# Attention output of an adaLN block: PV product in four column groups of 256 queries, normalised after a trip through DRAM

## The reference

```python
h = _layernorm(x) * (1 + ca) + sa
q, k, v = projections of h with bias, 16 heads of 16 features, q scaled by 0.25
scores = einsum('bihd,bjhd->bhij', q, k) + slopes * -|i - j|
probs = softmax(scores)                      # over the 1024 keys
out = einsum('bhij,bjhd->bihd', probs, v)    # the PV product
x = x + ga * (out @ Wo.T + bo)
h = _layernorm(x) * (1 + cb) + sb
x = x + gb * ffn(h)      # router over 16 experts, top 4, gate/up/down projections
```

## Time and profile before

| | us |
|---|---|
| three runs | 580.77, 583.66, 583.89 (median 583.66) |
| profiled execution, span from first to last instruction | 580.7 |
| profiled execution, own time | the page gives none beside the span |
| PE busy / DVE busy / ACT busy / POOL busy | 457.7 / 325.7 / 255.4 / 247.4 |
| mean granted TensorE clock | 0.901 of full |
| matmuls of PV, L1377, busy | 68.4 |
| matmuls of the merge, L1400, busy | 17.3 |

### The profile page before, as it was taken

How to read it: one execution, slowest core, us unless ns; L and a number is a source line. 1 busy time by engine, 2 the same in 40 slices (tenths; PEclk the granted TensorE clock), 3 DMA queues, 4 the chain that set the end, 5 groups by cost and what they waited for, 6 DMA issues and landing times.

```text
span 580.7 us, 9712 instructions
## 1 busy us (share of the span) xinstructions
PE 457.7 (79%) x2167; PEld 233.9 (40%) x2168; DVE 325.7 (56%) x1035; ACT 255.4 (44%) x407; POOL 247.4 (43%) x351
## 2 busy tenths in 40 slices
PE   4988689999999999999988637976787777677800
PEld 1673133333333333333436623644444444344400
DVE  3836988888888888888514592332232232322336
ACT  1365347677666666666774411322222222222211
POOL 4584954333333333332300004455555555555523
PEclk9798669999999999999998656999889899989965
DMA  8439274233322222233210201111111111122065
GB/s 227 186 82 316 73 266 142 84 95 94 91 91 91 89 94 93 95 96 88 72 34 2 73 1 41 51 57 58 54 61 47 55 55 52 57 63 46 19 197 165
DMA packets 29407, 53.02 MB, mean 91 GB/s; under 512 B 5144, under 2 KB 14030, under 8 KB 29383
## 3 DMA queue, kind: packets, MB, share of 16 engines
q1 hardware_dynamic: 20119, 30.35, 15.8%
q0 software_dynamic: 8720, 21.87, 13.0%
q10 hardware_dynamic: 544, 0.53, 0.3%
HBM read 38.47 MB, written 16.22 MB: 94 GB/s over the span
## 4 chain that ended last, share of the span: by engine, by line
PE 43%; issue 21%; DVE 12%; POOL 11%; DMA 7%; POOLq 2%; ACT 1%; SPq 1%; DVEq 0%; ACTq 0%
PE ps L1341 11%; PE ps L1377 10%; PE ps L1354 8%; POOL probs L883 7%; PE ps L1495 3%; PE ps L1400 3%; DVE junk L992 2%; PE ps L1236 2%; DMA probs<-xn_rows,probs 2%; DVE x_sb L1197 2%; DMA x_sb<-in_x 2%; POOL probs L880 1%; POOL z_rows L893 1%; DMA k_st<-z_rows 1%; POOL probs L890 1%
## 5 line engine op out<-in xcount | busy, mean ns | idle before, releaser
L992 DVE CUSTOM_DVE_ANT_0 junk<-ps,bias_t 128x512 bf16<-128x512 f32 x256 | 172.4, 687 | 49.2 <-PE ps L1341 47.4
L638 ACT ACTIVATE probs<-ps 128x1024 f32<-128x1024 f32 x128 | 130.4, 1025 | 80.5 <-DVE ps L1016 36.6
L1341 PE MATMUL ps<-k_st,q_st 96*128 96x512 bf16 x256 | 102.9, 405 | 19.0 <-DVE mx L992 12.3
L1495 PE MATMUL ps<-w_gu,probs 128*128 x188 | 86.8, 588 | 0.0
L1354 PE MATMUL ps<-q_st,k_st 123*128 123x512 bf16 x256 | 78.4, 388 | 1.6 <-DMA q_st<-m_rows 1.4
L1377 PE MATMUL ps<-probs,v_st 128*32 128x512 f32 x512 | 68.4, 607 | 0.6 <-ACT probs L638 0.6
L1182 DVE TENSOR_TENSOR probs<-probs,ps 128x224 f32<-128x224 f32 x47 | 18.2, 388 | 90.0 <-ACT probs L714 90.0
L1341 PEld LDWEIGHTS ps<-k_st,q_st 96*128 96x128 bf16 x256 | 26.1, 102 | 105.3 <-DVE mx L992 87.0
L883 POOL DMA_INDIRECT probs<-xn_rows,probs x47 | 48.7, 1035 | 41.8 <-POOL probs L880 31.0
L703 ACT ACTIVATE probs<-ps,modc 128x128 f32<-128x128 f32 x47 | 21.5, 457 | 102.0 <-PE ps L1479 102.0
L893 POOL DMA_INDIRECT z_rows<-probs x47 | 48.5, 1033 | 41.8 <-POOL probs L890 37.9
(11 more groups left out here) (195 smaller groups left out, 626.2 us busy)
## 6 DMA issues: line engine op xcount, KB each, us to landing
k_st<-k_rows SPq DMA_DIRECT2D x32, 192.0 KB
w_gu<-in_gate_proj POOLq DMA_DIRECT2D x16, 224.0 KB, 3.1
w_gu<-in_up_proj POOLq DMA_DIRECT2D x16, 224.0 KB, 3.5
w_dn<-in_down_proj POOLq DMA_DIRECT2D x16, 224.0 KB, 3.5
q_st<-q_rows SPq DMA_DIRECT2D x16, 192.0 KB
k_st<-z_rows SPq DMA_DIRECT2D x4, 512.0 KB, 5.8
al_rows<-w_gu SPq DMA_DIRECT2D x1, 1536.0 KB, 9.1
k_st<-al_rows SPq DMA_DIRECT2D x32, 48.0 KB
```

The costliest lines, as they stand in the source:

```text
L638: act.activation(probs[:, j % 4, :], ps_st[j % 2].rearrange("p b n -> p (b n)"), ACT.Exp).then_inc(exp_done, 1)
L992: dve.tensor_tensor_reduce(junk[:, half, :], ps_max[half], bias_t[:, g % 2, off:off + CH], 1.0, -3.0e38, ALU.add, ALU.max, mx[:, g % 2, q, ...
L1341: pe.matmul(ps_max[half], q_st[0:R_QK, s, q * P:q * P + P], k_st[0:R_QK, 0, s, CH * half:CH * half + CH], start=True, stop=True).then_inc( ...
L1495: last = pe.matmul(ps[:, 2 + c % 2, 0:2 * INTER], xT[:, c % 2, kk, :], w_gu[:, bass.ds(e, 1), kk, :].rearrange("p x n -> p (x n)"), start= ...
```

## The change: what it does

The PV product takes one key tile at a time: its four column groups are now four groups of 256 queries, and each group accumulates over all eight key tiles, so `ps_o` holds the finished sums in 128 partitions by 256 columns. `v_st` has 16 columns of ones in place of one, so that each group gives 16 rows of outputs and 16 equal rows of sums. There is no merge on PE and no normalise on DVE in the step. ACT copies 128x256 into one of two buffers; SP stores that to DRAM (`store_o`), and loads it back by half of the heads as `attT` (features on partitions, 1024 tokens) and `sums` in the same layout (`load_att`). DVE takes the reciprocal of all sums (a row for each feature) and multiplies. PE multiplies `attT` with Wo without a transpose. Heads 0 to 7 are one piece; heads 8 to 15 are normalised in four pieces of 256 tokens. The projection has four PSUM banks in place of three.

```diff
+G = 4
+QG = T // G
...
-        o_sb = sb("o_sb", [P, CH])
-        attn = sb("attn", [P, NCH, TC, E])
+        o_sb = sb("o_sb", [P, 2, QG])
+        attT = sb("attT", [P, KE, T])
+        sums = hT
...
+            def store_o(i, c):
+                sp.wait_ge(o_evac, at(i, c) + 1)
+                sp.dma_start(os_rows[at(i, c)].rearrange("r (g n) -> g r n", g=G), o_sb[:, c % 2, :]).then_inc(o_stored[c % 2], 16)
+            def load_att(k):
+                h = P // D
+                for s in range(2):
+                    sp.wait_ge(o_stored[s], 16 * (h // 2) * (k + 1))
+                for half, to in enumerate((sums, attT)):
+                    r = D * (1 - half)
+                    sp.dma_start(to[:, k, :], os_rows[h * k:h * k + h, r:r + D, :]).then_inc(att_in[k], 16)
...
                     load_qk(i, c + 3)
                     load_al(i, c + 3)
+                if output:
+                    store_o(i, c - 1)
...
             steps(sp, step)
+            load_att(0)
+            store_o(3, 3)
+            load_att(1)
...
-                if not (is0(i) and c == 0):
-                    act.wait_ge(ot_ready, at(i, c) + 1)
-                act.copy(o_sb[:], ps_o).then_inc(o_evac, 1)
+                if not (isinstance(i, int) and 4 * i + c < 2):
+                    act.wait_ge(o_stored[c % 2], (i * 2 + c // 2) * 16)
+                act.copy(o_sb[:, c % 2, :], ps_o[:, 0:QG]).then_inc(o_evac, 1)
...
-            pool.memset(v_st[:, :, :, D:D + 1], 1.0).then_inc(v_init, 1)
+            pool.memset(v_st[:, :, :, D:2 * D], 1.0).then_inc(v_init, 1)
...
-            def normalise(i, c):
-                ...
+            def normalise(k, first, last):
+                r = slice(first * P, last * P)
+                dve.reciprocal(sums[:, k, r], sums[:, k, r]).then_inc(sums_done[k], 1)
+                dve.wait_ge(sums_done[k], 1 if k == 0 else first // 2 + 1)
+                dve.tensor_tensor(attT[:, k, r], attT[:, k, r], sums[:, k, r], ALU.mult).then_inc(att_done, 1)
             steps(dve, step)
-            normalise(3, 3)
+            dve.wait_ge(att_in[0], 32)
+            normalise(0, 0, NT)
+            dve.wait_ge(att_in[1], 32)
+            for t in range(0, NT, 2):
+                normalise(1, t, t + 2)
...
-                    for ch in range(NCH):
-                        r = 32 * (2 * n + ch)
-                        last = pe.matmul(ps_o[r:r + 32], v_st[:, c % 2, j, :], probs[:, j % 4, CH * ch:CH * ch + CH],
-                                         start=(pair == 0), stop=(pair == 3))
+                    for g in range(G):
+                        last = pe.matmul(ps_o[32 * g:32 * g + 32, 0:QG], v_st[:, c % 2, j, :],
+                                         probs[:, j % 4, QG * g:QG * g + QG], start=(j == 0), stop=(j == NT - 1))
...
-            def merge_o(i, c):
-                ...
             steps(pe, step)
             sum_pv(3, 3, 3)
-            merge_o(3, 3)
...
...
+            for t in range(NT):
+                pe.wait_ge(att_done, 2 + t // 2)
+                if t >= 4:
+                    pe.wait_ge(x2_done, t - 3)
+                for k in range(KE):
+                    last = pe.matmul(ps[:, y1_banks[t % 4], 0:E], attT[:, k, t * P:t * P + P], wo_sb[:, k, :],
+                                     start=(k == 0), stop=(k == KE - 1))
+                last.then_inc(y1_ready, 1)
```

More of the change, by code:

```diff
@@ L24 @@
 D = E // H
-VW = D + 1
+G = 4
+QG = T // G
 CH = 512
@@ L74, in host_constants @@
     qrows = np.stack(rows * 3 + [r * (t % P) for r in rows] * 3)
[L75 to L78, removed]
     return {
@@ L86, in host_constants @@
         "triangle": bf16_bits(np.concatenate([np.triu(np.ones((P, P)), 1), np.ones((P, P))], 1)),
-        "route": np.concatenate([merge] + [np.broadcast_to(r, (P, r.shape[-1])) for r in (
+        "route": np.concatenate([np.broadcast_to(r, (P, r.shape[-1])) for r in (
             np.arange(NX), P * np.arange(NT), np.arange(NTAB), np.arange(P),
@@ L115, in adaln_block @@
         m_rows = dram("m_rows", [H, R_M, NT, P], BF16)
+        os_rows = dram("os_rows", [H, 2 * D, T], F32)
         xn_rows = dram("xn_rows", [T, E], F32)
@@ L173, in adaln_block @@
         triangle = sb("triangle", [P, 2, P], BF16)
-        route = sb("route", [P, NCH * VW + NX + NT + NTAB + P + 1 + NT * TOPK])
-        merge = route[:, 0:NCH * VW]
+        route = sb("route", [P, NX + NT + NTAB + P + 1 + NT * TOPK])
         dist = sb("dist", [P, W_DIST])
@@ L198, in adaln_block @@
         probs = sb("probs", [P, 4, T])
-        o_sb = sb("o_sb", [P, CH])
-        rsum = sb("rsum", [P, TC, NCH])
-        attn = sb("attn", [P, NCH, TC, E])
-        al_rest = attn[:].rearrange("p c t e -> p (c t e)")[:, 0:T]
+        o_sb = sb("o_sb", [P, 2, QG])
+        attT = sb("attT", [P, KE, T])
+        sums = hT
+        al_rest = attT[:, 0, :]
         xn = v_all
         late = carver(bias_t[:].rearrange("p s n -> p (s n)"))
-        attT = late([P, 3, KE, P])
         shift2 = late([P, TC])
@@ L262, in adaln_block @@
         ps_misc = ps[:, 7, :]
-        att_banks, y1_banks = (0, 1, 6), (2, 3, 7)
-        ps_ot = ps_misc[:, 0:TC * NCH * VW].rearrange("p (t c d) -> p t c d", t=TC, c=NCH)
+        y1_banks = (0, 1, 2, 3)
         x_in = [sem("x_in0"), sem("x_in1")]
@@ L323, in adaln_block @@
         o_evac = sem("o_evac")
-        ot_ready = sem("ot_ready")
-        ot_recip = sem("ot_recip")
-        ot_used = sem("ot_used")
+        o_stored = [sem("o_stored0"), sem("o_stored1")]
+        att_in = [sem("att_in0"), sem("att_in1")]
+        sums_done = [sem("sums_done0"), sem("sums_done1")]
+        att_done = sem("att_done")
         settled = sem("settled")
@@ L335, in adaln_block @@
         w_done = sem("w_done")
-        attT_ready = sem("attT_ready")
-        attT_evac = sem("attT_evac")
         y1_ready = sem("y1_ready")
@@ L502, in _ @@
             sp.wait_ge(qk_stored[1], 16 * 6)
+            def store_o(i, c):
[8 more added lines that the diff above has]
+                    sp.dma_start(to[:, k, :], os_rows[h * k:h * k + h, r:r + D, :]).then_inc(att_in[k], 16)
             def step(i, c):
-                _, rows, _, _ = kind(i, c)
+                _, rows, _, output = kind(i, c)
                 if not isinstance(i, int) or 2 <= 4 * i + c + 3 < H:
@@ L661, in _ @@
             evac_o(3, 3)
[L663 to L668, removed]
             def root(hf):
@@ L674, in _ @@
             call_table(ACT.Sqrt)
-            for t in range(6):
-                evac_att(t)
             root(0)
-            for t in range(6, NT):
-                evac_att(t)
             act.wait_ge(rstd2_done, 1)
@@ L911, in _ @@
             chain = [0]
-            dve.sem_inc(ot_used, 1)
             dve.memset(table_call[:, 0:1], 1.0).then_inc(preload, 1)
@@ L1006, in step @@
                         own_tile(i, c, q)
-                    if output and q == 6:
-                        normalise(i, c - 1)
             def own_tile(i, c, j):
@@ L1035, in split_rows @@
                  dve.tensor_tensor(part[:, 2, :], rest, part[:, 1, :], ALU.subtract)).then_inc(m_chain, 1)
-            def normalise(i, c):
[L1039 to L1046, removed]
-            steps(dve, step)
-            normalise(3, 3)
+            def normalise(k, first, last):
[3 more added lines that the diff above has]
+                dve.tensor_tensor(attT[:, k, r], attT[:, k, r], sums[:, k, r], ALU.mult).then_inc(att_done, 1)
+            steps(dve, step)
+            dve.wait_ge(att_in[0], 32)
[3 more added lines that the diff above has]
+                normalise(1, t, t + 2)
             dve.wait_ge(xg_done, 1)
@@ L1055, in residual @@
                 dve.wait_ge(y1_ready, t + 1)
-                dve.tensor_tensor(x_sb[:, t, :], ps[:, y1_banks[t % 3], 0:E], x_sb[:, t, :], ALU.add).then_inc(x2_done, 1)
+                dve.tensor_tensor(x_sb[:, t, :], ps[:, y1_banks[t % 4], 0:E], x_sb[:, t, :], ALU.add).then_inc(x2_done, 1)
                 dve.wait_ge(x2_done, t + 1)
@@ L1086, in _ @@
                                   ALU.subtract, ALU.mult).then_inc(xn_done[1], 1)
-            col = [NCH * VW]
+            col = [0]
             def consts(n):
@@ L1326, in step @@
                         rows_t(i, c + 1)
-                    if output and j == 5:
-                        merge_o(i, c - 1)
             def loaded(i, c):
@@ L1383, in rows_t @@
                 pe.wait_ge(m_chain, at(i, g, k=4) + 4)
-                if not (is0(i) and g < 2):
-                    pe.wait_ge(ot_used, at(i, g) - 1)
-                if is0(i) and g == 0:
+                if not (is0(i) and g == 0):
+                    pe.wait_ge(m_evac, at(i, g))
+                else:
                     pe.wait_ge(act_evac, count(Q0, "act"))
```

## The result

588.78 us after against 583.86 before (medians of 20 runs each): a ratio of 1.0082, 95% interval 1.0055 to 1.0109, so 4.8 us slower (3.2 to 6.4). The forecast was 587.2 us from 583.66, +3.5; the measured time also lies in the forecast's own range, 583 to 591. The span of the profiled execution went from 580.7 to 584.8.

A forecast was written before the change was run, and what follows sets the result against it. PE was taken to pace the heads, with a serial tail behind them. Heads 12.7 - 3.1 = 9.6 us shorter and tail 13.2 longer gave +3.6, so 587.2 us from 583.66, own range 583 to 591.

The forecast's parts named there:

- Merges, 12.7 us: Heads, on PE: removing the merge saves 0.91 us in each of 14 steps, 12.7 us, bounds 6.5 and 15.1.
- Rival C: Heads: freed PE time not won, as DVE or maxima rows pace the step; 0.35 less each, 592 us; 14%.
- Rounds of the PV product, +3.1: Heads, on PE: four rounds instead of two add 0.05 us per pair of key tiles, 3.1 us in all.
- the 13.8 that I had named as a sign of being wrong: Distance between heads: forecast to fall from 14.70 to 14.0 us; below 13.8 would show the prediction wrong.
- Rival D: PV product on PE: more, smaller matmuls in column groups don't overlap as well; slower; chance 6%.
- theory 3 of e5: PV product on PE: each instruction costs its own time, up to 0.15 us a pair, 9 us more in all.
- "Nothing is charged" for the maxima rows: Heads, SP's queue: the added store delays the maxima rows' DRAM trip at no cost, with 1.0 us slack left.
- Store to DRAM, 2.3 us: Tail: storing head 15's 128 KB output takes 2.3 us, so SP issues the reads 2.9 us after the copy.
- Reads, 4.6 us (4.2 to 5.6): Tail: two 512 KB reads back from DRAM take 4.6 us, so heads 8 to 15 are in SBUF at 7.5.
- Reciprocals, 8.3 ns an element: Tail, on DVE: each further element costs 8.3 ns, giving 8.67 us for 1024 elements and 2.27 for 256.
- Rival B: Tail, on DVE: the reciprocal streams like a plain operation; tail only +5.3 us, kernel 579.4 us; chance 12%.
- Residuals to normalised rows, 10.1 + 0.5: Tail's end, on DVE: residual additions, variance and normalised rows take 10.1 us, plus an added 0.5.

The follow-up runs named there:

- e5: Kernel before, merges kept, with only the PV product regrouped into four groups of 256 queries and ACT copying 128x256; 583.49 us, ratio 0.9995 to the kernel before.
- e2: Changed kernel with another layout of the DRAM copy, slowest dimension 8 for stores and 128 for reads; 582.17 us, ratio 0.9972 to the kernel before.
- e4: Changed kernel with the stores of head outputs issued by ACT on its DMA queue instead of SP's; 588.46 us, ratio 1.0097 to the kernel before.
- e1: Kernel before with the new PV product and two transposes in place of four merges, no DRAM trip; 572.33 us, ratio 0.9789 to the kernel before.
- e3: Changed kernel without the four reciprocals of heads 8 to 15; 584.91 us, ratio 1.0033 to the kernel before.

## Why the prediction was right

The sign, the place (saved in each head, paid back once behind them) and the size, +3.5 against +4.8 (3.2 to 6.4), came out. That the size is so close is in part luck: three costs were put too high (rounds, reciprocals, residuals) and three too low (store, reads, maxima rows), and they cancel.

- **Merges, 12.7 us.** Right. The distance between heads fell by 0.92, the full 0.91 of a merge; neither of the bounds (half of it, or 1.08) was needed. Rival C, which gave up 0.35 a step to DVE or the maxima rows, did not happen in the steady steps.
- **Rounds of the PV product, +3.1.** Wrong: 0. No run shows the 0.05 us a pair from which the 3.1 is made: it was my estimate for two more rounds, and in e5 a pair takes 1.00, as before. The forecast for a head, 14.0, was therefore 0.2 high, and the heads fell just below the 13.8 that I had named as a sign of being wrong (six of the eight steady distances are 13.77 to 13.79, two 13.82), for this reason. Rival D falls with it, as does theory 3 of e5: at 0.15 us a pair, which no run shows, the heads would be 9.6 longer than they are.
- **"Nothing is charged" for the maxima rows.** Right in the steady steps, where the slack was enough, and wrong in the last. In the last step the wait grew from 1.39 to 3.44, 0.9 of it foreseen (the merge of step 14 "brings nothing") and 1.2 not, and behind it two pairs of products took 1.03 and 1.06, at a granted clock of 0.50 (284.9 to 287.0), instead of the 0.60 of the earlier trace rows, where it was 1.00 (293.0 to 295.5). By e2 this cost 2.6. I had looked for queueing on SP, and e4 shows that the queue is not where it happens. Of the early distances between heads two gain only 0.65 and 0.03; that can't be put on the store, since e1, which has none, waits up to 1.16 for its maxima rows there. The very first distance, which is anything from 20.0 to 21.0 in these traces, is 1.0 longer. So -12.7 + 2.6 + 1.0 = -9.1, near the -9.3 measured. It stands next to the -9.6 of the sum because the 3.1 for rounds, which were free, happened to be about as large as what was left out.
- **Store to DRAM, 2.3 us:** 3.61. **Reads, 4.6 us (4.2 to 5.6):** 9.52, far outside the bounds. This is the step that failed. It took the price of a 512 KB read of another tile without asking at what share of the DMA engines either runs: 49.8% for the reads here, while in the trace before that read ran in packets of 1 KB with the DMA engines at nine tenths (558.3 to 561), as e2's do. With 128 outermost (e2) the reads take 5.24, inside the bounds; the 2.75 of its store is near the 2.3. So SP issues the reads 4.0 behind the copy and not 2.9, and they take 4.9 longer.
- **Reciprocals, 8.3 ns an element.** That a further element costs several times a plain one's was right, the size a third too large: 6553 and 1746 ns in these groups of DVE,

```profile
L1037 DVE RECIPROCAL hT<-hT 128x256 f32<-128x256 f32 x4 | 7.0, 1746 | 3.3 <-DMA attT<-os_rows 3.3
L1037 DVE RECIPROCAL hT<-hT 128x1024 f32<-128x1024 f32 x1 | 6.6, 6553 | 4.8 <-DMA attT<-os_rows 4.8
```

 which is (6553 - 1746) / 768 = 6.26 ns for each further element. Rival B would have needed less than 5.8, and with its plain-operation price (1.05 ns) it was off by six times. What makes an element of the reciprocal six times as dear is not shown. The four pieces took 8.50 after the data came, 2.4 less than the 10.9 forecast. The first piece ended 10.2 after the copy, 1.8 later than forecast, and it no longer mattered, since the reads took until 13.5. The chain was there, but behind another link than the one I put first, and PE was idle for 15.96 us ahead of its first projection product where I had 11.
- **Residuals to normalised rows, 10.1 + 0.5:** 9.76. No run shows the 0.5, which was my estimate of what the low clock of the projection would cost; that clock was there (0.50 from 312.7 to 317.0), hidden behind the reciprocals, as e3 shows by taking these away. That is why taking away 7.0 us of reciprocals brought 3.45.

The tail together, trace less forecast: 1.1 (store) + 4.9 (reads) - 0.9 (the first piece, now hidden) - 2.4 (pieces) - 0.8 (residuals) = +1.9, which is 31.8 against 29.9. The 16.7 itself holds some 1.5 of low clock (309 to 312) that the same tail in e5 did not have; against such a tail the change would be +16.6 and not +15.1.

## What to carry to other kernels

Work moved from inside a loop to behind it has to be priced at the full latency of each link, with idle engines and a fallen clock around it (granted 0.63 over this tail, 0.89 before): here savings of 0.9 us a head, 9.3 in all, lost against one trip of 13 us through DRAM and 8.5 us of reciprocals. Before pricing a transfer by another of the same size, compare the slowest dimension of each (the reads with 8 kept the DMA engines at 49.8%, with 128 at 100.7%). And look for the cheap middle: two transposes kept the reciprocal at 8 elements a partition, cost 0.3 us a head, and won 2.1% where the change as made lost 0.8%. The wide spread alone (e2) only brought the change back to the time of the kernel before.

## What the runs showed of the hardware that I had not expected

- Reads with 8 in their slowest dimension kept the DMA engines at 49.8%, with 128 at 100.7%; stores of the same packets went from 24.8% with 4 outermost to 41.5% with 8. The 1.05 MB of the reads took 9.5 and 5.2 us from first issue to use, although the second had packets a quarter the size.
- Float32 matmuls in four column groups: 16 of 256 columns take the 1.00 us of 8 of 512. The number of instructions in a column group was free at this size.
- A float32 transpose shows as one instruction where a float32 product shows as two (x2 for two transposes, x8 for four merges), and two of them cost 0.3 us between PV and scores.
- A 128 KB store that looked free on its own queue lengthened a 6 KB round trip by 1.2 us in the step where six weight loads also ran, whichever queue issued it; with 8 outermost in place of 4 it did not (3.26 against 3.27).
